# Unlimited early passes and a reordered second layer in a two-layer graph kernel

## The reference

```
h = x @ W + b_W;  xi, xj = split(h)
m = xj[src] + (edge_attr @ W_e + b_We)
m = m / (in_degree[dst] + 1e-6)
x1 = layernorm(x + xi + segment_sum(m, dst))            # layer 1

dinv = rsqrt(in_degree + 1)                             # self loops added
out = segment_sum((x1 @ W)[src+self] * dinv[src] * dinv[dst], dst+self) + b
y = (out - out.mean(0)) * rsqrt(out.var(0) + eps) * gamma + beta
x2 = layernorm(x1 + leaky(y))                           # layer 2
```

## Time and profile before

| | |
|---|---|
| runs | 1046.19, 1054.63, 1051.64 us; median 1051.64 us |
| profiled execution | 1049.88 us, its span 1048.0 us, mean granted clock 0.968 |
| busy, share of the span | PE 88%, PEld 78%, DVE 66%, ACT 45%, POOL 34% |
| stage one (up to the last `messages`) | 0 to 745.94 us |
| stage two (up to the last `weights`) | 745.94 to 999.06 us |
| DMA over the span | 247.94 MB, mean 237 GB/s |

### The profile page before, as it was taken

The page is one execution under the profiler, slowest core; times in us unless marked ns, Lnnn a source line. Parts: engine busy times, 40 slices in busy tenths (PEclk is TensorE's granted clock), DMA queues, the critical chain, the costliest instruction groups (busy, mean ns, idle before and its releaser), DMA issues. The chain is left out here.

```text
span 1048.0 us, 31421 instructions
## 1 busy us (share of the span) xinstructions
PE 927.3 (88%) x12418; PEld 817.7 (78%) x12418; DVE 689.9 (66%) x1690; ACT 466.4 (45%) x944; POOL 356.5 (34%) x492
## 2 busy tenths in 40 slices
PE   1579999999999999999999999999888898687755
PEld 0467898899888888888888988899777777566655
DVE  5997999999999888788888888883110001101046
ACT  1555666666566655555555655554200000000037
POOL 4565456655544344334443342321200001111100
PEclk9989999999999999999999999999999999989888
DMA  5569989888887777667677676760755765666434
GB/s 156 185 193 341 326 315 329 303 314 310 282 296 265 265 276 265 205 236 265 194 236 233 240 266 230 228 233 17 284 194 207 266 244 185 231 217 222 161 93 156
DMA packets 95685, 247.94 MB, mean 237 GB/s; under 512 B 41128, under 2 KB 63356, under 8 KB 89644
## 3 DMA queue, kind: packets, MB, share of 16 engines
q1 hardware_dynamic: 93132, 240.97, 66.1%
q0 software_dynamic: 2400, 4.88, 1.5%
HBM read 185.46 MB, written 60.35 MB: 235 GB/s over the span
## 5 line engine op out<-in xcount | busy, mean ns | idle before, releaser
L950 ACT CAST counts<-pair_ps 128x800 bf16<-128x800 f32 x391 | 319.2, 829 | 278.2 <-PE pair_ps L769 274.0
L547 DVE TENSOR_TENSOR lo_oh<-counter,lo_t 128x1024 bf16<-128x1024 bf16 x391 | 274.8, 703 | 79.5 <-PE pair_ps L769 76.5
L787 PE MATMUL x_ps<-counts,xsplit 128*128 128x256 bf16 (+1 forms) x2500 | 314.8, 270 | 3.2 <-issue 1.7
L787 PEld LDWEIGHTS x_ps<-counts,xsplit 128*128 128x128 f16 x2500 | 226.3, 97 | 36.6 <-issue 14.8
L550 DVE TENSOR_TENSOR key_oh<-counter,key_t 128x800 bf16<-128x800 bf16 x391 | 231.9, 593 | 0.0
L769 PE MATMUL pair_ps<-key_oh,lo_oh 128*128 128x100 bf16 x3128 | 207.9, 209 | 25.1 <-DVE key_oh L550 18.2
L769 PEld LDWEIGHTS pair_ps<-key_oh,lo_oh 128*128 128x128 bf16 x3128 | 182.4, 98 | 41.6 <-DVE key_oh L550 22.5
L736 DVE TENSOR_TENSOR s_mem<-pair_ps,early_in 128x256 f32<-128x256 f32 (+1 forms) x23 | 9.6, 418 | 195.8 <-PE pair_ps L855 195.8
L855 PE MATMUL pair_ps<-streams,zown 128*128 128x256 bf16 x904 | 114.6, 290 | 23.3 <-DMA streams<-counts_kept 19.2
L855 PEld LDWEIGHTS pair_ps<-streams,zown 128*128 128x128 f16 x904 | 93.0, 104 | 43.3 <-DMA streams<-counts_kept 20.9
L806 PE MATMUL e_ps<-streams 128*32 128x128 f32 x3528 | 110.7, 279 | 0.8 <-issue 0.8
(11 more groups left out here) (158 smaller groups left out, 924.5 us busy)
## 6 DMA issues: line engine op xcount, KB each, us to landing
streams<-in_edge_attr SPq DMA_DIRECT2D x196, 576.0 KB
counts_kept<-counts SPq DMA_DIRECT2D x10, 1664.0 KB, 9.3
streams<-counts_kept SPq DMA_DIRECT2D x6, 1664.0 KB, 9.0
counts<-counts_kept SPq DMA_DIRECT2D x4, 1664.0 KB, 9.3
counts_kept<-counts SPq DMA_DIRECT2D x2, 3200.0 KB, 13.3
streams<-counts_kept SPq DMA_DIRECT2D x2, 3200.0 KB, 15.5
dinv_row<-dinv_rows SPq DMA_DIRECT2D x25, 128.0 KB, 5.1
edst<-in_dst SPq DMA_DIRECT2D x196, 4.5 KB
```

What stands on the lines that cost most here:

```text
L547: dv.tensor_tensor(lo_oh[:, at % RING, :, :, :], counter[:, :, :].unsqueeze(1).to_broadcast([P, SW // 2, P, 2]), pairs(lo_t[b % 2][:, w]). ...
L787: last = nc.tensor.matmul(x_ps[:, 0, 0:n], xsplit[:, q // 2, q % 2, :], by_hi[:, q // 2, :], start=(q == 0), stop=(q == 2 * HI - 1))
L950: a.copy(out.rearrange("p h (g n) -> p h g n", g=2), pair_ps[at % 2][:, :, 0:4 * KW].rearrange("p g (n h) -> p h g n", h=HI)).then_inc(S[" ...
```

## The change

The cap on early passes goes: `early(k)` is 4 * (k - 1) up to 92 for block 24. `AGAIN` is 0, 23, 24 and then 1, 22, 2, 21, 3, 20, ... 11, 12, where it was 0, 23, 24, 1, 2, ... 22. The SP queue asks for table i + 3 in step i as the first thing, and for the early sum and dinv of step i + 1. The tables of steps 0 and 3 are asked for in iteration b = 24. VectorE's order in step i becomes `add_early(i)`, `scale_rows(i)`, statistics. A segment's statistics are taken as soon as its two blocks are there. `weights(i - 1)` stands after at most half the passes of step i.

```diff
-EARLY_MOST = 48
-AGAIN = [0, NB - 2, NB - 1] + list(range(1, NB - 2))
+AGAIN = [0, NB - 2, NB - 1] + [b for k in range(1, NB // 2) for b in (k, NB - 2 - k)]
 def early(k):
-    return min(4 * max(0, k - 1), EARLY_MOST)
+    return 4 * max(0, k - 1)
+def segments(i):
+    ready = lambda k, j: all(b in AGAIN[:j] for b in range(k * SEG // BN, (k * SEG + SEG - 1) // BN + 1))
+    return [k for k in range(NB) if ready(k, i + 1) and not ready(k, i)]
...
                 if early(b - 2):
                     keep_early(b - 2)
-                if b == NB:
+                if b == NB - 1:
                     load_counts(0)
                     load_counts(3)
+                if b == NB:
                     sp.dma_start(w1[:, :], keep["W1"]).then_inc(S["vectors_in"], 16)
...
+            load_early(1)
             for i in range(1, NB):
-                if i >= 4:
-                    load_counts(i)
-                if early(AGAIN[i]):
-                    load_early(i)
-                if i >= 2:
-                    load_inverse(i)
+                if i + 3 < NB:
+                    load_counts(i + 3)
+                if i + 1 < NB:
+                    if early(AGAIN[i + 1]):
+                        load_early(i + 1)
+                    load_inverse(i + 1)
...
             for i in range(NB):
-                if i + 1 < NB and early(AGAIN[i + 1]):
-                    add_early(i + 1)
+                if early(AGAIN[i]):
+                    add_early(i)
                 scale_rows(i)
                 dve.wait_ge(S["biased"], i + 1)
-                if AGAIN[i] == NB - 1:
-                    segment(NB - 1)
-                elif AGAIN[i] < NB - 2:
-                    segment(AGAIN[i])
-            segment(NB - 2)
+                for k in segments(i):
+                    segment(k)
             dve.wait_ge(S["counted"], NB)
...
                 first = early(AGAIN[i])
-                half = min(first + 20, 2 * HI)
+                half = first + min(20, (2 * HI - first) // 2)
                 gather_z(i, first, half)
                 weights(i - 1)
                 gather_z(i, half, 2 * HI)
```

## The result

The changed kernel took 998.68 us (median of 4, 995.61 to 1002.91), the kernel before 1052.96 us on the same chip (4 runs, 1046.19 to 1054.63): 0.950 of the time, 95% interval 0.944 to 0.956. The profiled execution took 995.61 us, its span 993.8. It was forecast at 987.4 and the median at 989, range 981 to 1003: 54.3 us came off, where 62.5 were forecast.

A forecast was written before the change was run, and what follows sets the result against it. TensorE bounds stage one; in stage two nothing is full and waits for loads cost time. Stage two -88.3, stage one +26.2, end -0.4: -62.5 us, so 1049.88 becomes 987.4, median 989, range 981 to 1003.

The forecast's parts named there:

- small loads that come late: Rival in stage two: early sums land behind large tables, late by some 1.5 us per pair; about 1000 us, 12 in 100.
- hand-overs in stage two: Range term: DVE and POOL hand-overs open by some 0.3 us in 25 steps, +7 us.
- TensorE bounds stage one; 264 passes cost 26.2 us there: Stage one, blocks 14 to 24: 264 more early passes cost 26.2 us, and stage two loses the same.
- That the spread puts 13 passes in a slot instead of 10 costs nothing extra.: Stage one's slots: 13 passes each cost nothing extra, as DVE has 4.5 us of room per block.
- Stage one grows by 26.2 us, since PE is its bound.: Stage one: growth is just the added passes' time, 24.0 us for 220 wide ones and 2.2 for 44 narrow ones.
- The waits for tables go, and with them the low clock.: Stage two: waits and the low clock behind them go, 253.1 to 164.8 us, -88.3 including the passes moved.
- 2.0 us for steps 1 and 2: Stage two: allowance of 2.0 us for the short steps 1 and 2 following each other.
- Long and short blocks in turn keep DMA hidden.: Stage two: each pair of blocks takes PE 13.5 us and keeps DMA busy 10.4, so loads stay hidden.
- `weights(1)` waits 1.3 us, step 2 may cost 0.7.: Stage two's start: `weights(1)` waits about 1.3 us for its sum; step 2's early sum may cost 0.7 more.
- The end gains 0.4 us: Last step: its scaling no longer stands behind step 23's scaling, bias and statistics, gaining 0.4 us.
- the clock did not stay low: Rival in stage two: the clock stays low though the waits go, costing 20 us; about 1010 us, 3 in 100.
- the loads do overlap: Rivals in stage two: loads do not overlap, about 1044 us, 3 in 100; the slower side, 1070 us, 2 in 100.

The follow-up runs named there:

- run 1: Kernel before with only the loads asked for ahead (tables three steps, early sum and dinv one): 992.94 us, ratio 0.946.
- runs 7 and 8: Changed kernel with passes spread evenly and the store behind the edge rows: with the cap of 48 986.10 us (0.954), without it 986.67 us (0.952).
- run 4: Changed kernel with the passes spread evenly over slots 1 to 15, without rounding up: 987.98 us, ratio 0.941.
- runs 9 and 12: Changed kernel with a block's first edge sums in slot 6 instead of 5, 1001.47 us (0.954); changed kernel again, 998.93 us (0.953).
- run 3: Changed kernel with the cap of 48 early passes back, all else kept: 987.01 us, ratio 0.942.

## Why the prediction was right, and where it was off

The median of 998.68 us lies inside the range, but 9.7 us above the forecast, and not for a reason that the range was made for. It kept room for small loads that come late and for hand-overs in stage two. The loss came in stage one, for which it had no term. That it fell inside is luck in part.

*TensorE bounds stage one; 264 passes cost 26.2 us there.* Right: 25.2 us in the sums by series (26.2 against run 1, without the gap of before), and 26.2 in the pair of runs 7 and 8.

*"That the spread puts 13 passes in a slot instead of 10 costs nothing extra."* The first step that failed. I looked at the full slots and at DVE's room, not at the empty ones that rounding up leaves at the end of a block. There PE is not the bound but waits for ScalarE's copies. 3.7 us, shown by run 4.

*"Stage one grows by 26.2 us, since PE is its bound."* The term was mis-sized also by what it left out. I took a bound engine to be a sum of durations. Inserted passes also shift what comes later against the other engines, here the edge series against GpSimd's gathers, by 0.3 to 1.1 us in seven of eight blocks. That is 10.6 us in the edge sums, less 4.0 that the same gaps had cost in the x sums. That the position decides is shown by runs 9 and 12; what makes the gaps is open. The rows that would have warned stood in the trace of before: the gaps at 604.70 and 606.22.

*The waits for tables go, and with them the low clock.* Right, to 0.3 us in 254.6, although 0.8 of the 2.0 us for steps 1 and 2 did not come, so small terms offset each other. The causal account was too narrow: I named the `scale_rows` behind the next sum as what holds the SP queue, and then credited the loads three ahead alone. Moving the scaling removes the same cause. Alone the two bring stage two to 191.9 and 195.4 us. Their gains don't add.

*Long and short blocks in turn keep DMA hidden.* True but not needed: run 1 in rising order had no wait for a table, and run 3 none with the cap. DMA was busy at 0.74, near the forecast (10.4 of 13.5, which is 0.77).

*`weights(1)` waits 1.3 us, step 2 may cost 0.7.* The first was 1.18, the second did not show. *The end gains 0.4 us:* it lost 0.1. The time from the last `weights` to the end lies between 48.7 and 50.8 us in the runs, so this term can't be read.

*The rivals.* No small load came late, the clock did not stay low, the loads do overlap. The figure of the Trainium skill ("DMA: Bandwidth & Descriptors", Specifications: about 358 GB/s from HBM to one core) decided nothing here: stage two's mean of 272 GB/s lies below it. It is no ceiling for this kernel, though, for the stretch of the earlier trace rows ran at 422.

## What to carry to other kernels

When a queue asks for loads too late, look for what it stands behind: here a wait for a small operation of VectorE, ordered behind a large one. Reordering that operation and asking further ahead each cure it, and are not to be counted twice. Work moved from a stage to another that the same engine bounds gains nothing by itself; it costs what it does to the evenness of the slots and to the meeting of the engines, so spread it to the last slot and compare starts, not busy time.

## What the runs showed of the hardware that was not expected

- PE has gaps, most of them of 0.15 to 0.35 us, that nothing in the profile explains, 1.3 to 3.2 us after the start of the first of two indirect gathers on GpSimd. In a series of 128x32 f32 weight loads with matmuls every 29 ns the two or three gaps cost 1.5 to 2.2 us, in a series at 109 ns 0.4 to 0.9. Behind the third gather of a block there are none, and on one of the chips used they are absent.
- The kernel before took 1052, 1034 and 1050 us on the three chips. The changed kernel itself ran in the first comparison and on the third chip, both times beside 1050 to 1053 us for the kernel before. Its ratio on the chip of 1034 us, where the gaps are absent, stays open.
